# Codes of four later chunks from the normalised tokens in place, with twice scaled weights

## The chip, the cores and the metric

The kernel runs on one core of one Trainium2 chip. The metric is the device time of one execution in microseconds (us); lower is better. TensorE, VectorE, ScalarE, GpSimd and SyncE are called PE, DVE, ACT, POOL and SP in the profile. PEld is TensorE's weight loading, which runs beside its products.

## The reference, cut to what matters

The input is normalised, and then goes through an RWKV-6 attention layer and a mixture of experts; both results are added to the input. The part that the change touches is the start of the attention layer, the low-rank codes:

```
xn     = layernorm(x)                      # 4 x 1024 tokens, 256 channels
x_last = concatenate([zeros, xn[:, :-1]])  # the token before
b_a    = x_last - xn
xx     = xn + b_a * miu_x                  # mixed tokens
h      = tanh(xx @ A).reshape(5, B * T, 32)
```

`A` has 256 rows and 160 columns (five groups of 32). The reshape lays the products out so that token t's five codes come from different tokens. Everything behind `h` (five mixtures, decay, key, value, receptance, gate, the recurrence, the output and the experts) is left as it is.

## The kernel before, in words

The normalised tokens lie in SBUF with channels on the partitions, in two halves of 128 channels (`xnT`, a view of `xnf`), each sequence with a zero column ahead of it. The attention part goes through eight chunks of 128 tokens, each in two units of two sequences; a unit is written (u, c). Each engine has its own program, a list of steps written out by hand, and semaphores order the engines against each other. An engine takes its steps strictly in the written order. The first stretch, to about 130 us, interleaves the codes of all chunks with the units (0,0), (1,0) and (0,1) and with the routing of tokens to experts; behind it the loop `half` takes one unit and its share of the 39 expert tiles per turn.

The codes of chunk c go as follows.

- ACT, `scaled(c)` (L1355): two instructions, one for each half of the channels, write `xn * (1 - miu_x)` for 20 strips of 28 tokens (560 columns) into one of two buffers `xxb`. It waits for the products of the chunk before last (`s["hm"]`).
- DVE, `shifted(c)` (L845): two instructions add `x_last * miu_x` in place. That makes the mixed tokens of the chunk.
- ACT, `codes(c)` (L1383 and L1388): tanh into `codes_f`, then a rounded copy into `codes_hl`.
- DVE, `low_codes(c)` (L866): the remainder of the rounding. SP then writes the codes to memory, from where they are loaded for each unit.

The other steps that the prediction speaks of: on PE `mixed(u, c, n)` (L435) forms the five mixtures' factors from the codes, `decay_down` (L446), `decay_up` (L459), `key` (L466, `wk`), `value` (L482), `receptance` (L466, `wr`), `gate_down` (L498), `first_levels` (L515), `middle_levels` and `last_levels` (L525, L556), `key_back` (L570), `read_out` (L590, L594), `state` (L605), `table` (L406), `gated_back` (L630). On DVE `mixed` (L1024) and `added` (L1032) form the mixtures, `grow` (L1085 to L1087) and `levels` (L1054, L1063) belong to the recurrence, `places_of_tiles` (L964 to L978) and `at_rows` (L982) to the routing, `key` is L1040. On ACT `decay_down` is L1411, `decay` L1419 and `gate_down` L1442.

The order around the change, on PE: `first_levels(0,0)`, `mixed(1,0,1)`, `codes(3)`, `decay_down(1,0)`, `mixed(1,0,2)`, `decay_up(1,0)`, `middle_levels(0,0)`, `key(1,0)`, `codes(4)`, `mixed(1,0,3)`, `value(1,0)`, `last_levels(0,0)`, `mixed(1,0,4)`, `receptance(1,0)`, `codes(5)`, `gate_down(1,0)`, `mixed(0,1,0)`, `first_levels(1,0)`, `mixed(0,1,1)`, `key_back(0,0)`, `codes(6)`, `decay_down(0,1)`, `state(0,0)`, `mixed(0,1,2)`, `read_out(0,0)`, `codes(7)`, `decay_up(0,1)`, `table(0)`.

The waits of `codes(c)` on PE, and the view of the strips:

```
def tokens_of(c, cc, shift):
    at = PAD + cc * ROWS + BASE[c] + shift - 1
    return xnf[:, at:at + NB * (T + 1)].rearrange("p (s n) -> p s n", n=PITCH)[:, :, 0:SEG]
...
pe.wait_ge(s["xx"], c + 2)
...
    pe.wait_ge(s["h"], c if c > 5 else c - 1)
```

`SEG` is 28 and `PITCH` 205: a chunk's strips are 20 runs of 28 tokens, 205 apart. `wA` lies in `z`, `xxb` and the codes' buffers in the first part of `w1`, which holds the experts' first weights later. Their load (SP, L1889) waits until all codes are written out.

Of the kernel before, what the change touches and what calls it, by code (L numbers as in the profile page):

```python
# [11 lines left out]
ACT = mybir.ActivationFunctionType  # L12
AX = mybir.AxisListType

P = 128
NB, T, C = 4, 1024, 256
TOK = NB * T
CC = C // P
# [52 lines left out]

NSEG, PITCH, SEG = NB * NS, (NB * (T + 1)) // (NB * NS), 28
SHIFT = [4 + (P * c - 4) % NS for c in range(NCH)]
BASE = [(P * c + NS - f) // NS for c, f in enumerate(SHIFT)]
# [24 lines left out]
def program(nc, io):  # L101
    with ExitStack() as ctx:
        def sb(name, shape, dt=F32):
# [77 lines left out]

        s = {n: ctx.enter_context(nc.semaphore("s_" + n)) for n in (

            "cv cn c1 c2 w x0 x1 x2 x3 x4 x5 x6 x7 xk ck0 ck1 ck2 z_pool omx bn ag ve rs nm xna xnd xnp tr tc sc lg xx hm h hi lo "
            "four hg hf hc cx ls lgc lgt bst cst wvc ew1 ew2 "

            "step exp cnt slot att ohp inv back srow drow ex "
# [13 lines left out]
        def cvec(col, cc):  # L201
            return vec[:, col + cc:col + cc + 1]
# [30 lines left out]
        HAT = FAT + 2 * TC5  # L233
        codes_f = [w1[:, FAT + TC5 * k:FAT + TC5 * (k + 1)] for k in range(2)]
        codes_hl = [w1[:, HAT + 2 * NS * P * k:HAT + 2 * NS * P * (k + 1)].rearrange("p (x i n) -> p x i n", x=2, i=NS) for k in range(3)]
        lgs = w1s[:, 0, :, :].rearrange("p k n -> p (k n)")[:, 0:NT * E]
        wA = flat(z)[:, 0:CC * GR].rearrange("p (c n) -> p c n", c=CC)
        wA4 = D[:, :, :].rearrange("p u n -> p (u n)")[:, 0:CC * GR * 4].rearrange("p (a m) -> p a m", m=P)
# [22 lines left out]
# [4 lines that stand above are left out]
        def codes_in(c, cc):  # L265
            return xxb[c % 2][:, cc, :].rearrange("p (s n) -> p s n", n=SEG)

        def half_of(strips, u):
            return strips.rearrange("p (s b) n -> p s b n", b=NB)[:, :, UB * u:UB * (u + 1), :]
# [27 lines left out]
        def home(c):  # L297
            return YB if c in (0, 2, 4) else F2
# [36 lines left out]
        def tensor_program(pe):  # L335
# [41 lines left out]

            def codes(c):

                pe.wait_ge(s["xx"], c + 2)  # L380
                if c == 0:
                    pe.wait_ge(s["hf"], 2)
                elif c == 1:
                    pe.wait_ge(s["hf"], NS)
                else:
                    pe.wait_ge(s["h"], c if c > 5 else c - 1)
                for g in range(NS):
                    for cc in range(CC):
                        for t in range(NB):
                            i1 = pe.matmul(home(c)[LORA * t:LORA * (t + 1), g * GAP:g * GAP + GSEG], wA[:, cc, LORA * g:LORA * (g + 1)],  # L390
                                           xxb[c % 2][:, cc, t * GSEG:(t + 1) * GSEG], start=(cc == 0), stop=(cc == 1), tile_position=(0, LORA * t))
                i1.then_inc(s["hm"])

            def counts():
# [424 lines left out]
        def vector_program(dve):  # L819
# [21 lines left out]

            def shifted(c):
                for cc in range(CC):
                    dve.wait_ge(s["sc"], CC * (c + 1) + cc + 1)
                    i1 = dve.scalar_tensor_tensor(codes_in(c, cc), tokens_of(c, cc, 0), cvec(MX, cc), codes_in(c, cc), ALU.mult, ALU.add)  # L845
                i1.then_inc(s["xx"])

# [381 lines left out]
            tiles_of_experts()  # L1229
            mixed(1, 0, 0)  # L1230
            low_codes(2)
            shifted(3)
            grow(0, 0, 1)
            dve.wait_ge(s["z_pool"], 3)
            levels(0, 0, 0)
# [5 lines left out]
            mixed(1, 0, 2)  # L1241
            grow(0, 0, 4)
            low_codes(3)
            shifted(4)
            grow(0, 0, 8)
            added(1, 0, 2)
            levels(0, 0, 2, 3)
# [14 lines left out]
            slots()  # L1262
            low_codes(5)
            mixed(0, 1, 0)
            shifted(6)
            added(0, 1, 0)
            gate_terms(1, 0)
            mixed(0, 1, 1)
            places_of_tiles()
            low_codes(6)  # L1270
            shifted(7)
            added(0, 1, 1)
            mixed(0, 1, 2)
            at_rows(0)
# [59 lines left out]
        def scalar_program(act):  # L1334
# [7 lines left out]
            def columns(j):  # L1342
                act.wait_ge(s["tr"], j + 1)
                for cc in range(CC):
                    i1 = act.activation(xrow(j, 1)[:, cc, :], pair_of(j)[cc][:, :], ACT.Copy)
                i1.then_inc(s["tc"])
# [10 lines left out]
            def scaled_half(u):  # L1357
                act.wait_ge(s["tc"], NJ - 1 + u)
                act.wait_ge(s["xna"], NJ - 1)
                act.wait_ge(s["xnd"], NJ - 1)  # L1360
                act.wait_ge(s["xnp"], NJ - 1)
                for cc in range(CC):
                    act.activation(half_of(codes_in(0, cc), u), half_of(tokens_of(0, cc, 1), u), ACT.Copy, scale=omx[:, cc:cc + 1]).then_inc(s["sc"])

            def four_copies():
                act.wait_ge(s["c1"], 48)
# [39 lines left out]
            def decay_down(u, c):  # L1406
                q = seq(u, c)
                act.wait_ge(s["tA"], q + 1)
                if q:
                    act.wait_ge(s["tB"], q)  # L1410
                act.activation(tw[:, :], bank(u, c, "tw")[:, 0:P], ACT.Tanh).then_inc(s["tw"])  # L1411
# [203 lines left out]
            scaled(1)  # L1615
            act.wait_ge(s["w"], 208)
            decay_down(0, 0)
            decay(0, 0)
            exponentials()
            codes(1)  # L1620
# [3 lines left out]
            receptance(0, 0)  # L1624
            bonus(0, 0)
            codes(2)
            scaled(3)
            gate_down(0, 0)
            saved(0, 0, 2)
            saved(0, 0, 4)  # L1630
            codes(3)
            decay_down(1, 0)
            scaled(4)
            decay(1, 0)
            saved(0, 0, 16)
            saved(0, 0, 32)
# [5 lines left out]
            receptance(1, 0)  # L1642
            bonus(1, 0)
            codes(5)
            scaled(6)
            gate_down(1, 0)
            spread(0, 0)
            key_back(0, 0)
            codes(6)
            scaled(7)  # L1650
            decay_down(0, 1)
            squares(0, 0)
            codes(7)
# [308 lines left out]
```

## Time and profile before

| | us |
|---|---|
| median of 3 runs | 579.27 (577.48 to 579.47) |
| the profiled execution, its own time | 581.6 |
| its span in the profile | 580.3 |
| PE busy | 527.7 (91% of the span) |
| PEld busy | 469.8 (81%) |
| DVE busy | 449.1 (77%) |
| ACT busy | 338.5 (58%) |
| POOL busy | 195.1 (34%) |

The span runs from the first to the last instruction; the execution's own time is 1.3 us longer. Busy time is the union of an engine's instructions. In a row of the timeline, instructions that follow each other on one line are merged: the columns are start, duration, engine, line, operation, output and inputs, count, and in brackets the idle time ahead of them with what ended it. A merged row's end can reach past the next row's start, since instructions overlap in the pipeline. In a row of a window, the granted TensorE clock stands behind the engines' busy times: 1.00 is 2.4 GHz, 0.50 is 1.2 GHz.

### The profile page before, as it was taken

The numbers are of one execution on the slowest core, as the hardware profiler recorded it, in microseconds if no ns is written. First come the engines' busy times: TensorE is split into PE (matmuls) and PEld (weight loads), VectorE is DVE, ScalarE is ACT, GpSimd is POOL, SyncE is SP. The second block draws the span as 40 slices with busy tenths as digits, with TensorE's granted clock in tenths as the row PEclk, the third lists the DMA queues.
The fourth block names the chain that finished last, engine by engine and source line by source line (L and its number), as shares of the span: only waits on it lengthen the run. The fifth ranks groups of instructions, "written<-read, shape, count | busy, mean of one in ns | idle before, by whom it ended". The sixth has DMA issues, their size and how long they took to land. (4 is left out here: it accounts for less than half of the span.)

```text
span 580.3 us, 19573 instructions
## 1 busy us (share of the span) xinstructions
PE 527.7 (91%) x7662; PEld 469.8 (81%) x7662; DVE 449.1 (77%) x1116; ACT 338.5 (58%) x753; POOL 195.1 (34%) x156
## 2 busy tenths in 40 slices
PE   2879796987999999999999899999998999989984
PEld 2667586876898999998998799999997889878873
DVE  6879999977869596968697787869676868878552
ACT  4975564324575756566666557575746666565751
POOL 7901010130324334434243232524333523423332
PEclk9999899997999999999999999999999999999999
DMA  8989654579332434324233323242433433221323
GB/s 281 265 298 306 171 137 102 148 274 322 88 72 39 96 47 94 56 75 75 73 62 89 46 72 51 57 81 43 99 47 75 74 76 56 48 38 39 38 39 46
DMA packets 49805, 60.80 MB, mean 105 GB/s; under 512 B 5057, under 2 KB 44098, under 8 KB 49570
## 3 DMA queue, kind: packets, MB, share of 16 engines
q1 hardware_dynamic: 36898, 44.72, 27.0%
q0 software_dynamic: 11840, 14.42, 16.6%
q8 instruction: 62, 1.02, 0.8%
q10 hardware_dynamic: 976, 0.41, 0.3%
q14 instruction: 29, 0.24, 0.1%
HBM read 40.79 MB, written 23.07 MB: 110 GB/s over the span
## 5 line engine op out<-in xcount | busy, mean ns | idle before, releaser
L1742 POOL DMA_INDIRECT out<-rows,dst_row x39 | 63.9, 1637 | 214.3 <-DVE rows L1153 187.6
L661 PE MATMUL F<-xsT,w1s 128*128 128x128 f32 x624 | 76.8, 276 | 2.5 <-issue 1.4
L661 PEld LDWEIGHTS F<-xsT,w1s 128*128 128x128 f32 x624 | 74.7, 192 | 4.8 <-issue 1.8
L1024 DVE SCALAR_TENSOR_TENSOR mix<-G,vec,ba 128x256 f32<-128x256 f32 x160 | 69.6, 477 | 11.4 <-PE G L435 11.3
L669 PE MATMUL F<-w,hsT 128*128 x312 | 75.1, 383 | 0.5 <-ACT hsT L1542 0.3
L1542 ACT ACTIVATE hsT<-F,b1c 128x128 f32<-128x128 f32 x156 | 44.4, 369 | 35.3 <-PE F L661 31.4
L669 PEld LDWEIGHTS F<-w,hsT 128*128 128x128 f32 x312 | 57.2, 190 | 8.8 <-issue 0.9
L1063 DVE COPY_PREDICATED AP_<-msk,LL 128x256 f32<-128x256 uint32 x96 | 51.2, 534 | 16.3 <-issue 11.0
L1085 DVE TENSOR_TENSOR RK<-RK,D 128x256 f32<-128x256 f32 x112 | 47.4, 423 | 19.0 <-issue 10.7
L1032 DVE TENSOR_TENSOR mix<-mix,xnT 128x512 f32<-128x512 f32 x80 | 55.1, 688 | 1.5
L1728 POOL DMA_INDIRECT rows<-xn_d,src_row x39 | 40.8, 1046 | 33.5 <-PE F L650 16.6
L1153 DVE SCALAR_TENSOR_TENSOR rows<-F,of_row,b2t 128x256 f32<-128x256 f32 x39 | 18.6, 477 | 41.3 <-PE F L669 41.2
L1086 DVE TENSOR_TENSOR RK<-RK,D 128x256 f32<-128x256 f32 x112 | 46.9, 419 | 0.0
L1535 ACT ACTIVATE w1s<-w 128x1024 f32 x39 | 41.7, 1069 | 3.5 <-issue 3.5
L435 PE MATMUL G<-cd,bst 128*128 128x256 f32 x160 | 40.2, 338 | 1.9 <-ACT tg L1442 1.0
L1720 POOL TENSOR_TENSOR gn<-gn,small 128x8 f32<-128x8 f32 x16 | 28.3, 1771 | 39.0 <-DVE gn L1120 38.9
L1466 ACT ACTIVATE D<-RK 128x256 f32<-128x256 f32 x32 | 13.8, 430 | 41.7 <-DVE D L1087 41.6
L1716 POOL TENSOR_TENSOR ba<-xnT 128x512 f32<-128x512 f32 x16 | 18.4, 1152 | 55.7 <-DVE mix L1024 55.5
L1524 ACT ACTIVATE xsT<-F 128x256 f32<-128x256 f32 x39 | 14.9, 381 | 31.8 <-PE F L650 31.4
L466 PE MATMUL G<-mix,wk 128*128 128x256 f32 x128 | 31.4, 389 | 2.2 <-ACT D L1419 2.2
L482 PE MATMUL G<-wv,mix 128*128 128x256 f32 x128 | 30.6, 381 | 2.8 <-DVE RK L1040 2.8
L1748 POOL DMA_DIRECT2D out<-res x16 | 21.2, 1326 | 34.4 <-DMA out<-rows,dst_row 34.4
(181 smaller groups left out, 1216.0 us busy)
## 6 DMA issues: line engine op xcount, KB each, us to landing
cd<-cd_d SPq DMA_DIRECT2D x30, 320.0 KB, 5.2
w<-in_W SPq DMA_DIRECT2D x16, 512.0 KB, 8.9
cd_d<-w SPq DMA_DIRECT2D x32, 160.0 KB, 2.8
b2t<-in_b SPq DMA_DIRECT2D x39, 128.0 KB
w<-in_x SPq DMA_DIRECT2D x8, 512.0 KB, 9.5
xn_d<-w SPq DMA_DIRECT2D x8, 512.0 KB
out<-in_x SPq DMA_DIRECT2D x8, 512.0 KB, 5.8
out<-res POOLq DMA_DIRECT2D x16, 256.0 KB
```

The source lines that it names most:

```text
L435: i1 = pe.matmul(bk[:, cc * UN:(cc + 1) * UN], bst[:, n, cc * P:(cc + 1) * P], cd[:, u, n, :].bitcast(F32R), start=True, stop=True)
L661: i1 = pe.matmul(FB[:, k * P:(k + 1) * P], w1s[:, cc, k, :], xsT[:, cc, :], start=(cc == 0), stop=(cc == 1))
L669: i1 = pe.matmul(FB[:, 0:C], hsT[:, k, :], w2[:, bass.ds(number[f] * (HC * C) + k * C, C)], start=(k == 0), stop=(k == HC - 1))
L1024: i1 = dve.scalar_tensor_tensor(mixed_in(u, c, n, cc), bk[:, cc * UN:(cc + 1) * UN], cvec(LAM + CC * n, cc), ba[:, cc, :, :].rearrange("p ...
L1032: dve.tensor_tensor(buf, buf, xunit(u, c, 1), ALU.add).then_inc(s["x"])
L1063: dve.copy_predicated(to, m, now.rearrange("p g (n t) -> p g n t", t=B)).then_inc(s["a"])
L1085: dve.tensor_tensor(r2, r2, bcast(tt[:, :, 0], B), ALU.mult)
L1086: dve.tensor_tensor(k2, k2, bcast(tt[:, :, 1], B), ALU.mult)
L1535: act.activation(w1s[:, :, :, :].rearrange("p c k n -> p (c k n)"), w1[:, bass.ds(n * (CC * HID), CC * HID)], ACT.Copy).then_inc(s["fw"])
L1542: i1 = act.activation(hsT[:, k, :], FB[:, k * P:(k + 1) * P], ACT.Relu, bias=b1c[:, bass.ds(number[f] * HC + k, 1)])
L1728: pool.indirect_dma_start(xs[:, f % 2, :], None, xn_d, bass.IndirectOffsetOnAxis(src_row[:, f:f + 1], 0)).then_inc(s[f"xs{f % 2}"], 16)
L1742: pool.indirect_dma_start(io["out"], bass.IndirectOffsetOnAxis(dst_row[:, f:f + 1], 0), ys[:, f % 2, :], None, compute_op=ALU.add).then_in ...
```

## The change

For the chunks 3, 4, 6 and 7 (`DIRECT`) no mixed tokens are formed. The sum `xn * (1 - miu_x) + x_last * miu_x` is not taken before the product but in it: `wA` is kept in two more versions, `wAs`, one scaled by `miu_x` and one by `1 - miu_x`, and PE multiplies the first with the strips one token back and the second with the strips themselves, both read from the normalised tokens in place. An accumulation group has four products where it had two, so such a chunk has 80 matmuls (160 records) where it had 40 (80). The chunks 1, 2 and 5 (`STRIPS`) and chunk 0 stay as they are. `scaled` and `shifted` of the four chunks are gone from ACT and DVE; `weights_of_strips` is new on ACT, with four instructions between `decay_down(0, 0)` and `decay(0, 0)`. No DMA, no step of POOL and no step of SP changes.

```
+DIRECT = (3, 4, 6, 7)
+STRIPS = [c for c in range(1, NCH) if c not in DIRECT]
...
+        SAT = HAT + 3 * 2 * NS * P
+        wAs = w1[:, SAT:SAT + 2 * CC * GR].rearrange("p (x c n) -> p x c n", x=2, c=CC)
...
-                pe.wait_ge(s["xx"], c + 2)
+                if c in DIRECT:
+                    pe.wait_ge(s["ws"], 2 * CC)
+                else:
+                    pe.wait_ge(s["xx"], 3 + STRIPS.index(c) if c else 2)
...
-                for g in range(NS):
-                    for cc in range(CC):
-                        for t in range(NB):
-                            i1 = pe.matmul(home(c)[LORA * t:LORA * (t + 1), g * GAP:g * GAP + GSEG], wA[:, cc, LORA * g:LORA * (g + 1)],
-                                           xxb[c % 2][:, cc, t * GSEG:(t + 1) * GSEG], start=(cc == 0), stop=(cc == 1), tile_position=(0, LORA * t))
+                def columns(w, of, n):
+                    for g in range(NS):
+                        for m in range(n):
+                            for t in range(NB):
+                                i1 = pe.matmul(home(c)[LORA * t:LORA * (t + 1), g * GAP:g * GAP + GSEG], w(m)[:, LORA * g:LORA * (g + 1)],
+                                               of(m, t), start=(m == 0), stop=(m == n - 1), tile_position=(0, LORA * t))
+                    return i1
+
+                if c in DIRECT:
+                    i1 = columns(lambda m: wAs[:, m // CC, m % CC, :], lambda m, t: tokens_of(c, m % CC, m // CC)[:, NS * t:NS * (t + 1), :], 2 * CC)
+                else:
+                    i1 = columns(lambda m: wA[:, m, :], lambda m, t: xxb[c % 2][:, m, t * GSEG:(t + 1) * GSEG], CC)
                 i1.then_inc(s["hm"])
...
-                    dve.wait_ge(s["sc"], CC * (c + 1) + cc + 1)
+                    dve.wait_ge(s["sc"], CC * (2 + STRIPS.index(c)) + cc + 1)
...
             low_codes(2)
-            shifted(3)
             grow(0, 0, 1)
...
             low_codes(3)
-            shifted(4)
             grow(0, 0, 8)
...
             mixed(0, 1, 0)
-            shifted(6)
             added(0, 1, 0)
...
             low_codes(6)
-            shifted(7)
             added(0, 1, 1)
...
+            def weights_of_strips():
+
+                for cc in range(CC):
+                    act.activation(wAs[:, 0, cc, :], wA[:, cc, :], ACT.Copy, scale=cvec(MX, cc)).then_inc(s["ws"])
+                    act.activation(wAs[:, 1, cc, :], wA[:, cc, :], ACT.Copy, scale=omx[:, cc:cc + 1]).then_inc(s["ws"])
...
             decay_down(0, 0)
+            weights_of_strips()
             decay(0, 0)
...
             codes(2)
-            scaled(3)
             gate_down(0, 0)
...
             decay_down(1, 0)
-            scaled(4)
             decay(1, 0)
...
             codes(5)
-            scaled(6)
             gate_down(1, 0)
...
             codes(6)
-            scaled(7)
             decay_down(0, 1)
```

How the change stands on the engines, at two places. On PE, from `mixed(1,0,1)` to the start of `decay_down(1,0)`, with the products of chunk 3 between; before:

```order
L435 MATMUL G<-cd,bst 128x256 [waits s_tg]
L435 MATMUL G<-cd,bst 128x256
L390 MATMUL F<-w,z 32x140 [waits s_h,s_xx]
L390 MATMUL F<-w,z 32x140 x39
L446 MATMUL G<-mix,tdA 64x128 [waits s_m,s_x]
```

and with the change:

```order
L449 MATMUL G<-cd,bst 128x256 [waits s_tg]
L449 MATMUL G<-cd,bst 128x256
L398 MATMUL F<-xnT,w 32x140 [waits s_h,s_ws]
L398 MATMUL F<-xnT,w 32x140 x79
L460 MATMUL G<-mix,tdA 64x128 [waits s_m,s_x]
```

The step stands where it stood, has twice as many matmuls, reads `xnT` with the weights in `w`, and waits no longer for DVE (`s_xx`) but for the scaled weights (`s_ws`). The other three chunks read alike.

On DVE, around `places_of_tiles` and the strips of chunk 7 (L845 here), before:

```order
L974 TENSOR_TENSOR w<-rows,placef 128x32x39 [waits s_tr,s_xk,s_slot]
L976 TENSOR_TENSOR w<-w,prob 128x32x39 [waits s_att]
L978 TENSOR_TENSOR w<-w,rows 128x32x39 [waits s_att]
L866 TENSOR_TENSOR w<-w 128x640 [waits s_ck0,s_hi]
L845 SCALAR_TENSOR_TENSOR w<-xnT,vec,w 128x560 [waits s_sc] x2
L1032 TENSOR_TENSOR mix<-mix,xnT 128x512 [waits s_m]
```

and with the change (lines are 14 further down):

```order
L988 TENSOR_TENSOR w<-rows,placef 128x32x39 [waits s_tr,s_xk,s_slot]
L990 TENSOR_TENSOR w<-w,prob 128x32x39 [waits s_att]
L992 TENSOR_TENSOR w<-w,rows 128x32x39 [waits s_att]
L880 TENSOR_TENSOR w<-w 128x640 [waits s_ck0,s_hi]
L1046 TENSOR_TENSOR mix<-mix,xnT 128x512 [waits s_m]
```

Only the two instructions on the strips are gone; what stood behind them follows directly. All steps that stay keep their order on every engine.

## Rows read from the trace of the kernel before

**Rows 1.** The page's part 1: busy time of each engine over the whole span.

```profile
PE 527.7 (91%) x7662; PEld 469.8 (81%) x7662; DVE 449.1 (77%) x1116; ACT 338.5 (58%) x753; POOL 195.1 (34%) x156
```

**Rows 2.** Windows: stretch, its length, busy PE, PEld, DVE, ACT, POOL, granted clock, DMA.

```profile
60.27:103.41 43.14, 35.08 (x758) 29.83 (x762) 41.42 (x83) 21.89 (x41) 1.55 (x1) 0.92 0.50 133
69.00:73.00 4.00, 4.00 (x96) 3.62 (x90) 3.47 (x8) 1.21 (x4) 0.00 (x0) 0.57 0.61 132
104.90:126.60 21.70, 20.17 (x238) 18.24 (x238) 21.07 (x50) 6.85 (x17) 3.25 (x3) 1.00 0.82 256
133.00:134.00 1.00, 1.00 (x14) 1.00 (x16) 1.00 (x4) 0.47 (x1) 0.00 (x0) 0.50 1.04 367
220.00:280.00 60.00, 60.00 (x859) 54.62 (x859) 46.49 (x115) 38.16 (x89) 22.15 (x17) 1.00 0.36 71
```

**Rows 3.** Timeline of PE around the products of the chunks 3, 4, 6 and 7.

```profile
60.27 0.50 PE L435 MATMUL G<-cd,bst 128*128 128x256 f32 x2 [0.48 <-ACT tg L1442]
61.64 2.59 PE L390 MATMUL F<-w,z 128*32 128x140 f32 x80 [0.86 <-DVE w L845]
65.53 0.66 PE L446 MATMUL G<-mix,tdA 128*64 128x128 f32 x8 [1.30 <-DVE mix L1032]
67.92 0.67 PE L459 MATMUL G<-tw,tdB 64*64 64x128 f32 x16 [1.10 <-DVE mix L1024]
...
73.75 2.47 PE L390 MATMUL YB<-w,z 128*32 128x140 f32 x76
...
76.27 0.51 PE L435 MATMUL G<-cd,bst 128*128 128x256 f32 x2
...
90.35 2.59 PE L390 MATMUL F<-w,z 128*32 128x140 f32 x80 [1.23 <-DVE w L845]
92.87 0.66 PE L446 MATMUL G<-mix,tdA 128*64 128x128 f32 x8
...
95.97 0.40 PE L594 MATMUL YB<-V,AT 128*64 128x64 f32 x8
99.18 4.23 PE L390 MATMUL F<-w,z 128*32 128x140 f32 x80 [2.80 <-DVE w L845]
```

**Rows 4.** Timeline of DVE: strips of chunk 3, and the waits behind it.

```profile
60.07 1.51 DVE L845 SCALAR_TENSOR_TENSOR w<-xnT,vec,w 128x560 f32<-128x560 f32 x2
61.50 0.42 DVE L1085 TENSOR_TENSOR RK<-RK,D 128x256 f32<-128x256 f32 x1
...
76.82 0.88 DVE L1024 SCALAR_TENSOR_TENSOR mix<-G,vec,ba 128x256 f32<-128x256 f32 x2 [0.48 <-PE G L435]
...
103.36 0.42 DVE L1087 TENSOR_TENSOR D<-D 128x256 f32<-128x256 f32 x1
105.00 0.83 DVE L866 TENSOR_TENSOR w<-w 128x640 fp32r<-128x640 f32 x1 [1.22 <-ACT w L1388]
...
129.81 0.43 DVE L1085 TENSOR_TENSOR RK<-RK,D 128x256 f32<-128x256 f32 x1 [3.24 <-PE LL L525]
```

**Rows 5.** Timeline of ACT: the place of the new instructions, and steps near the change.

```profile
40.75 0.28 ACT L1411 ACTIVATE tw<-G 128x128 f32<-128x128 f32 x1 [0.24 <-PE G L446]
43.06 0.84 ACT L1419 ACTIVATE D<-G,vec 128x256 f32<-128x256 f32 x2 [2.04 <-PE G L459]
...
58.31 1.43 ACT L1355 ACTIVATE w<-xnT,small 128x560 f32<-128x560 f32 x2
59.64 0.58 ACT L1442 ACTIVATE tg<-G 128x512 f32<-128x512 f32 x1
...
103.45 0.75 ACT L1383 ACTIVATE w<-F 128x700 f32<-128x700 f32 x1 [6.43 <-PE F L390]
104.23 0.74 ACT L1388 ACTIVATE w<-w 128x640 fp32r<-128x640 f32 x1
```

**Rows 6.** Timeline of PE: products whose moving operand is in one run, and in pieces of 8.

```profile
149.81 0.65 PE L525 MATMUL LL<-Ru,AT 64*64 64x32 f32 x32
150.28 0.65 PE L525 MATMUL LL<-RK 64*64 64x32 f32 x32
```

More of the change, by code:

```diff
@@ L182, in program @@
         s = {n: ctx.enter_context(nc.semaphore("s_" + n)) for n in (
-            "cv cn c1 c2 w x0 x1 x2 x3 x4 x5 x6 x7 xk ck0 ck1 ck2 z_pool omx bn ag ve rs nm xna xnd xnp tr tc sc lg xx hm h hi lo "
+            "cv cn c1 c2 w x0 x1 x2 x3 x4 x5 x6 x7 xk ck0 ck1 ck2 z_pool omx bn ag ve rs nm xna xnd xnp tr tc sc ws lg xx hm h hi lo "
             "four hg hf hc cx ls lgc lgt bst cst wvc ew1 ew2 "
```

## The prediction

> **What bounds the kernel now.** The page's part 1 comes first: over the whole span PE is busy for 91% [rows 1]. Then the windows, since that share is an average [rows 2]. From 220 to 280 us PE is busy for all of 60.00 us while DVE has 46.49: the loop behind the change is bound by PE, so whatever moves the loop's start moves the end by as much. The stretch with the four products, from 60.27 to 103.41 us, is another matter: PE is busy for 35.08 of 43.14 us, DVE for 41.42. Part of PE's work there also runs slowly: from 69 to 73 us the granted clock is 0.57 on average. Behind it, from 104.90 to 126.60, DVE is busy for 21.07 of 21.70 us and sets the pace.
>
> The timeline of PE shows what the 8.06 us of idle PE were waiting for [rows 3]. The products of chunk 3 waited 0.86 us for the strips from DVE, those of chunk 6 1.23, those of chunk 7 2.80. Those of chunk 4 did not wait. Between them PE waited for DVE's mixtures (1.30 and 1.10 us) and twice about half a microsecond for ACT's gate tanh (0.48 in the row, once more ahead of chunk 6). So this stretch is a loop of dependencies between PE and DVE in which both are nearly full, and the change moves work from the fuller of the two to the other.
>
> **What it adds.** A chunk's 80 records take 2.59 us at full clock [rows 3], 32.4 ns each, and the next step starts as they end (76.27, 92.87). So a direct chunk takes 160 records, 5.18 us, and four of them add 4 x 2.59 = 10.4 us to PE. No row shows this product with its moving operand read in runs of 28. I price it at 32.4 ns. The other end is 52.9 ns, from the 4.23 us of chunk 7 at reduced clock.
>
> **What it takes away.** On DVE a pair of strip instructions keeps the engine for 61.50 - 60.07 = 1.43 us [rows 4]; four pairs are 5.7 us. On ACT a pair is 1.43 busy, with the gate tanh starting 1.33 us behind its start [rows 5]; four pairs are 5.3 us. ACT is not full, so only the two places count where the tanh stood behind a pair, chunks 3 and 6.
>
> **The scaled weights.** Four ACT instructions of 128x160. The nearest rows are 0.28 us for 128x128 and 0.42 each for the pair of 128x256, so 1.1 to 1.7 us, and they go into the 2.04 us in which ACT waits for PE between L1411 and L1419 [rows 5]. Cost zero; without this cover `decay(0,0)`, and PE's `key(0,0)` behind it, would come up to 1.7 us later. The wait on `ws` is over some 15 us before chunk 3.
>
> **The stretch, step by step** (before, then after, in us).
>
> - Chunk 3. Without `scaled(3)`, ACT's tanh is no longer late, PE's `mixed(1,0,1)` starts at 59.8 instead of 60.27 and the products at 60.3 instead of 61.64. They end at 65.5 instead of 64.2. DVE, 1.4 us earlier, has the mixture for `decay_down(1,0)` ready at 64.1, so this starts at 65.5, as before (65.53). `decay_up(1,0)` waits for `mixed(1,0,2)` on both engines and comes at 67.5 instead of 67.92. The doubled products have filled PE's waits.
> - The clock. From 69 to 73 us the mean grant was 0.57 [rows 2], so 0.43 x 4.00 = 1.7 us of full-speed work were lost. PE had been idle for 3.3 us of the 8 before (the three waits above). With the direct products those 8 us have some 1.5 idle, and I take it that the clock stays up. From `decay_up(1,0)` to the products of chunk 4 it was 73.75 - 67.92 = 5.8 us; less 1.7 that is 4.1, from 67.5 to 71.6.
> - Chunk 4 had no wait to fill [rows 3]: 71.6 to 76.8, where it ended at 76.3. So `mixed(1,0,3)` comes 0.5 us late. DVE waited for it even before (0.48 at 76.82 [rows 4]); now it waits over 2 us, which is where the time won from chunks 3 and 4 on DVE is lost again. From there to the strips of chunk 6 both engines run 0.5 us late.
> - Chunk 6. DVE drops a pair and is 0.9 us ahead. On PE, `mixed(0,1,1)` no longer waits for the tanh, so the lag of 0.5 is gone and `key_back` ends at 89.1. The products start at 89.1 instead of 90.35 and end at 94.3 instead of 92.9. PE is 1.4 us late: the step behind `read_out` can start at 97.5 instead of 96.15 (95.97 plus the 0.2 us after which a row's last products let the next step begin, as the rows around them show).
> - Chunk 7 starts there, at 97.5 instead of 99.18. Before, it fell to half clock right behind the 2.80 us of waiting, and took 4.23 us. With no wait ahead of it I take full clock: 5.18 us, ending at 102.7 instead of 103.41.
> - Next in line are ACT's two steps (L1383, L1388; rows 5) and DVE's `low_codes(7)`, which waited 1.22 us for them at 105.00 [rows 4]. They come 0.7 us earlier. DVE, which gets there at 101.4 rather than 103.8 (+0.5 of lag, -2.9 for the pairs of chunks 6 and 7), spends the rest waiting. From here DVE sets the pace to 126.6, the writing of chunk 7's codes and the loading of the experts' weights behind it follow, and the whole shifts by -0.7.
>
> As a sum over PE: 10.4 added; 4.9 of waits for strips, 1.0 of waits for the tanh and 1.9 of other waits filled; 1.7 and 1.6 of clock given back (4.23 - 2.59). That leaves -0.7. The span becomes 580.3 - 0.7 = 579.6, with the 1.3 us around it 580.9, against 581.6 of the profiled execution. That execution was 2.3 us over the median of 579.27; against the median the forecast is **578.6**. A measurement of this kernel tells about 0.5% (2.9 us) from no change.
>
> **A rule weighed.** In 60.27 to 103.41 PEld is busy for 29.83 us (69%), PE for 35.08, DVE for 41.42 (96%) [rows 2]. The Trainium skill, Perfetto Trace Analysis, Identifying the Most-Contended Engine, says that matmul busy time does not tell how near TensorE is to its limit, that weight loading's busy share should be read for it, and that the engine with the highest occupancy is to be relieved first. By that TensorE has room, the change relieves the right engine and the sum would be near -5.7 instead of -0.7. The trace speaks against the room: the products of a chunk and the step behind them stand end to end [rows 3].
>
> **The rivals.**
>
> - **The clock stays low.** The half-speed stretches have another cause than PE's waits, and come back at the same length: 1.7 and about 1.6 us lost again. Then chunk 4 ends at 78.5 and the end is at -0.7 + 3.3 = +2.6, which is 581.9. For it: the first fall came behind waits of 1.30 us at most, the second behind 2.80. Against: from 220 to 280 us, with PE full, the grant is 1.00 throughout.
> - **The direct products cost more per record (slower).** The place is the 640 direct records. Each ns on top of 32.4 adds 0.64 us to PE, since nothing is left to fill; from 33.5 ns on the change loses, from 38 ns by over 0.5% (3.6 us / 640). At the bound of 52.9 ns it is 13.1 us, so 578.6 + 13.1 = 591.7. For it: the moving operand comes in runs of 28 from four places at once. Against: the recurrence's products with a moving operand in pieces of 8 take the 0.65 us of those in one run [rows 6].
> - **DVE is the bound** and PE takes the added records between others: -5.7, 573.6. It needs room on PE that the end-to-end steps don't show.
> - **A later stretch goes another way.** At 133 us the clock is at half again, and DVE waits 3.24 us for PE at 129.81 [rows 2, 4]. If the shift spares that, some 2 to 3 us go with it: about 576. Equally it could lengthen.
> - That the change doesn't do what it says: the order shows the eight DVE instructions gone and 80 matmuls in four places, so no chance is kept for it.
>
> **How the numbers follow.** Forecast 0.58. The clock stays low 0.15, of which 0.03 end above +0.5% (where it comes back longer). Direct records dearer 0.15, slower. DVE the bound 0.06, faster. A later stretch 0.06, faster. So faster 0.12, same 0.58 + 0.12 = 0.70, slower 0.18. The range reaches down to the forecast less the spread of the runs and part of the last rival, 575.8, and up past the low clock, 582.8. Outside are the bound by DVE and most of the dearer records.
>
> **What would show it.** Right: 160 records in 5.2 us for each of the four chunks, no waits for DVE ahead of them, a granted clock of 1.00 from 60 to 103 us, chunk 4's products ending about 0.5 us later and chunk 7's about 0.7 earlier than before, a new DVE wait of over 2 us for PE near 75 and one near 102. Wrong: a direct chunk above 6 us at full clock, grants near 0.5 inside 60 to 103, or a loop that starts more than 3 us from where it did.

## The result and the profile after

The changed kernel takes 584.17 us (median of 4 runs, 583.56 to 586.42) against 578.77 of the kernel before beside it (4 runs, 577.48 to 579.47). The ratio is 1.0089, with a 95% interval from 1.0052 to 1.0127: **slower by 0.9%**, 5.4 us, where 578.6 had been forecast. In a second comparison (e5, below) it was 1.0073 (1.0042 to 1.0105). The profiled execution took 584.46 us for a span of 583.2. Medians in us are over all executions; a ratio leaves out those over 1.5% above the fastest of the same kernel (two of six in e1, one of six in e2).

Part 1 of the page after, beside [rows 1]: PE has 320 records more and 7.5 us more of busy time, DVE 5.3 us less, ACT 3.6 less.

```profile
PE 535.2 (92%) x7982; PEld 476.5 (82%) x7982; DVE 443.8 (76%) x1108; ACT 334.9 (57%) x749; POOL 195.7 (34%) x156
```

ACT's timeline shows the four scaled weights (L1378, L1379) in the wait that had been named for them [rows 5]. Of the wait 0.77 us are left, so they cost nothing.

```profile
41.34 0.28 ACT L1427 ACTIVATE tw<-G 128x128 f32<-128x128 f32 x1 [0.24 <-PE G L460]
41.51 0.42 ACT L1378 ACTIVATE w<-z,vec 128x160 f32<-128x160 f32 x1
...
42.47 0.41 ACT L1379 ACTIVATE w<-z,small 128x160 f32<-128x160 f32 x1
43.66 0.84 ACT L1435 ACTIVATE D<-G,vec 128x256 f32<-128x256 f32 x2 [0.77 <-PE G L473]
```

PE's timeline after, beside [rows 3]. The direct products are the rows of L398 with x160.

```profile
44.64 3.55 PE L480 MATMUL G<-mix,wk 128*128 128x256 f32 x8 [1.04 <-ACT D L1435]
...
61.18 0.89 PE L529 MATMUL LL<-Ru,RK 64*64 64x96 f32 x32
...
62.43 5.37 PE L398 MATMUL F<-xnT,w 128*32 128x140 f32 x160
67.73 0.66 PE L460 MATMUL G<-mix,tdA 128*64 128x128 f32 x8
...
71.61 0.67 PE L539 MATMUL LL<-RK 64*64 64x32 f32 x30
74.25 0.24 PE L539 MATMUL LL<-RK 64*64 64x32 f32 x2 [1.97 <-issue]
74.42 2.70 PE L480 MATMUL G<-mix,wk 128*128 128x256 f32 x8
77.05 6.03 PE L398 MATMUL YB<-xnT,w 128*32 128x140 f32 x160
83.01 0.50 PE L449 MATMUL G<-cd,bst 128*128 128x256 f32 x2
...
95.22 5.13 PE L398 MATMUL F<-xnT,w 128*32 128x140 f32 x160
100.28 0.66 PE L460 MATMUL G<-mix,tdA 128*64 128x128 f32 x8
...
103.72 5.11 PE L398 MATMUL F<-xnT,w 128*32 128x140 f32 x160
108.77 0.67 PE L473 MATMUL G<-tw,tdB 64*64 64x128 f32 x16
```

Two things are to be seen. No direct product waits for anything, and at full clock 160 records take 5.11 to 5.37 us. And in the middle levels (L539) PE stands for 1.97 us between the 30th and the 31st of 32 records, with nothing named that it waited for. The windows after give the clock: half at 45 to 48 us and again from 75.5 to 79, right behind that standstill, in which no engine did anything (73 to 74).

```profile
45.00:48.00 3.00, 3.00 (x9) 2.34 (x8) 1.72 (x4) 0.42 (x1) 0.00 (x0) 0.50 1.32 343
60.27:69.00 8.73, 8.55 (x209) 7.12 (x207) 7.41 (x18) 4.06 (x9) 0.00 (x0) 1.00 0.75 217
73.00:74.00 1.00, 0.00 (x0) 0.00 (x0) 0.00 (x0) 0.00 (x0) 0.00 (x0) 1.00 0.21 51
75.50:79.00 3.50, 3.50 (x41) 2.42 (x43) 3.40 (x9) 1.44 (x4) 0.00 (x0) 0.51 0.61 176
```

DVE's timeline, beside [rows 4], has the two new waits that were forecast, at 83.55 and 110.48, and ahead of them a third of 3.33 us, for the products at which PE stood.

```profile
74.60 0.42 DVE L1099 TENSOR_TENSOR RK<-RK,D 128x256 f32<-128x256 f32 x1 [3.33 <-PE LL L539]
...
83.55 0.88 DVE L1038 SCALAR_TENSOR_TENSOR mix<-G,vec,ba 128x256 f32<-128x256 f32 x2 [3.87 <-PE G L449]
...
110.48 0.82 DVE L880 TENSOR_TENSOR w<-w 128x640 fp32r<-128x640 f32 x1 [2.68 <-ACT w L1404]
```

This last instruction stood at 105.00 before: 5.5 us late. They add up as follows. `first_levels` started at 61.18 instead of 58.90: +2.3. Of that 0.6 stood already at 41 us (ACT's tanh at 41.34 instead of 40.75 [rows 5]), and 1.7 are the half clock behind it, in `key(0, 0)` at 44.64 above all (3.55 us for its 8 records). From there to `decay_up(0, 1)` it was 44.4 us before (58.90 to 103.33), 43.7 by the forecast (58.9 to 102.6), and 47.6 after: 3.9 more than forecast. The standstill is 1.97 of that, the half clock from 75.6 to 79.0 another 1.7.

That these 5.5 us are as large as the difference of the medians is chance. The two profiled executions differ by 2.9 us at their end (spans of 583.2 and 580.3), since the kernel before lost more behind it: from 126 to 142 us its granted clock was 0.79 on average, and 0.89 after, which is 3.4 against 1.8 us of full-speed work. The rows are the kernel before and the changed one.

```profile
126.00:142.00 16.00, 12.00 (x215) 10.50 (x215) 8.82 (x26) 5.87 (x12) 3.60 (x3) 0.79 0.90 276
126.00:142.00 16.00, 12.59 (x188) 10.96 (x187) 11.47 (x33) 6.93 (x15) 3.60 (x3) 0.89 0.79 229
```

### The profile page after: what moved, and what is told of

Same layout as the page of the kernel before. It is cut to its first block and busy times, and to the rows that moved or that the text cites. A ratio compares the mean times of both kernels' runs of the same rounds, so it can differ in the third digit from the quotient of the medians.

```text
span 583.2 us, 20201 instructions
## 1 busy us (share of the span) xinstructions
PE 535.2 (92%) x7982; PEld 476.5 (82%) x7982; DVE 443.8 (76%) x1108; ACT 334.9 (57%) x749; POOL 195.7 (34%) x156
## 3 DMA queue, kind: packets, MB, share of 16 engines
q8 instruction: 64, 1.05, 0.8%
## 5 line engine op out<-in xcount | busy, mean ns | idle before, releaser
L675 PE MATMUL F<-xsT,w1s 128*128 128x128 f32 x624 | 76.9, 276 | 2.1 <-ACT xsT L1540 1.4
L675 PEld LDWEIGHTS F<-xsT,w1s 128*128 128x128 f32 x624 | 74.7, 192 | 4.7 <-ACT xsT L1540 1.6
L683 PE MATMUL F<-w,hsT 128*128 x312 | 75.2, 383 | 0.6 <-ACT hsT L1558 0.3
L683 PEld LDWEIGHTS F<-w,hsT 128*128 128x128 f32 x312 | 57.1, 190 | 9.1 <-issue 1.2
L1558 ACT ACTIVATE hsT<-F,b1c 128x128 f32<-128x128 f32 x156 | 44.4, 368 | 34.8 <-PE F L675 34.7
L1167 DVE SCALAR_TENSOR_TENSOR rows<-F,of_row,b2t 128x256 f32<-128x256 f32 x39 | 18.6, 477 | 43.5 <-PE F L683 43.5
L480 PE MATMUL G<-mix,wk 128*128 128x256 f32 x128 | 33.0, 404 | 2.2 <-ACT D L1435 2.2
L651 PE MATMUL YB<-wo,sq 128*128 128x256 f32 x128 | 30.7, 381 | 2.2 <-issue 1.5
```

The costliest lines, as they stand in the source:

```text
L675: i1 = pe.matmul(FB[:, k * P:(k + 1) * P], w1s[:, cc, k, :], xsT[:, cc, :], start=(cc == 0), stop=(cc == 1))
L683: i1 = pe.matmul(FB[:, 0:C], hsT[:, k, :], w2[:, bass.ds(number[f] * (HC * C) + k * C, C)], start=(k == 0), stop=(k == HC - 1))
L1558: i1 = act.activation(hsT[:, k, :], FB[:, k * P:(k + 1) * P], ACT.Relu, bias=b1c[:, bass.ds(number[f] * HC + k, 1)])
```

## The experiments

In all of them the edit is against the changed kernel, whose diff stands above.

### The two halves of the change, each alone (e1, e2)

**e1** lets each accumulation group of a direct chunk stop after two of its four products, so the codes of the chunks 3, 4, 6 and 7 lack the part of the tokens themselves: DVE and ACT are relieved, and PE keeps its 80 records per chunk.

```
-                    i1 = columns(lambda m: wAs[:, m // CC, m % CC, :], lambda m, t: tokens_of(c, m % CC, m // CC)[:, NS * t:NS * (t + 1), :], 2 * CC)
+                    i1 = columns(lambda m: wAs[:, m // CC, m % CC, :], lambda m, t: tokens_of(c, m % CC, m // CC)[:, NS * t:NS * (t + 1), :], CC)
```

> The changed kernel with the products of chunks 3, 4, 6 and 7 cut to half (80 records a chunk, those with the token before alone; the half with the token itself is left out). ACT and DVE are relieved as in the change, PE has no added records. Working theory (VectorE's 5.7 us come back where it sets the pace, and PE's added 10.4 us are what eats them): 3 to 6 us faster than the kernel before, no wait of these products for DVE, no idle of PE marked issue around 72 us. Rival (the stretch is bound by PE and by fixed points such as the routing, so relief alone brings nothing): within 1 us of the kernel before.

Measured: 575.93 us against 580.33 (ratio 0.9893, 0.9843 to 0.9942). The stretch from `first_levels` to `decay_up(0, 1)` takes 37.3 us. The direct form with one run of 80 records takes 2.67 us, as the products of strips do, and PE waits for DVE again behind it:

```profile
61.73 2.67 PE L398 MATMUL F<-xnT,w 128*32 128x140 f32 x80
65.67 0.66 PE L460 MATMUL G<-mix,tdA 128*64 128x128 f32 x8 [1.26 <-DVE mix L1046]
```

**e2** forms and awaits the strips of all chunks as before, and multiplies the four chunks directly all the same.

```
-DIRECT = (3, 4, 6, 7)
+DIRECT = ()
...
-                if c in DIRECT:
+                if c in (3, 4, 6, 7):
...
+            shifted(3)
...
+            scaled(3)
...
```

`shifted` and `scaled` of the chunks 4, 6 and 7 come back in the same way, and so do the waits of `codes` on `xx`.

> The kernel before with only PE's side of the change: direct products with 160 records for chunks 3, 4, 6 and 7, but the strips are still formed and still waited for, and the scaled weights are made. Working theory: the added records have no wait left to fill, so 8 to 11 us slower than before, less what DVE works on meanwhile; at the least 5. Rival (PE has room for the records between others, as the low share of weight loading would have it): within 2 us of before.

Measured: 588.32 us, 1.0118 (1.0079 to 1.0156), and 52.6 us for the stretch. The waits for strips stay and the long products come on top. PE's rows for the chunks 3 and 6:

```profile
62.77 5.46 PE L398 MATMUL F<-xnT,w 128*32 128x140 f32 x160 [0.81 <-DVE w L859]
...
98.60 5.13 PE L398 MATMUL F<-xnT,w 128*32 128x140 f32 x160 [1.22 <-DVE w L859]
```

So the change is a trade of two effects of several microseconds each: -4.4 us for the relief and +8.0 for the records by the medians, -6.2 and +6.8 by the ratios. PE did not take the added work for free. The rule of the Trainium skill (Perfetto Trace Analysis, Identifying the Most-Contended Engine), by which PEld's 69% left room on TensorE, would have given -5.7. e2 speaks against that room: with the waits for strips kept, the added records cost 6.8 to 8.0 us.

### Which chunks lose (e3, e11, e4, e7)

`DIRECT` says which chunks are direct; `scaled` and `shifted` of the others stand where they stood before. **e3**, and again **e11**: the chunks 6 and 7. **e4**: chunk 4. **e7**: chunk 3.

```
-DIRECT = (3, 4, 6, 7)
+DIRECT = (6, 7)
```

> Direct products for the chunks 6 and 7 alone; 3 and 4 as before. Both had waits for strips (1.23 and 2.80 us) and chunk 7 ran at half clock behind its wait (1.6 us lost), so by the step-by-step working 5.2 us are added and 5.6 + 0.5 taken away: 0 to 2 us faster than before. Theory that the loss sits in chunks 3 and 4 (a record more without a wait to fill, the idle issue of 2 us and the slow clock behind it): this kernel is at least 4 us faster than the changed one. Rival (the direct products cost their full time wherever they are): 2.5 us slower than before.

> The kernel with direct products for chunks 6 and 7 alone once more, on another visit, to see whether it beats the kernel before: it gave 0.996 (0.993 to 0.999). Theory 'waits filled': the two chunks filled 4.0 us of PE's waits of 5.2 added, and freed DVE and ACT, so 0.993 to 0.999 again. Rival 'the visit': the clock's falls and the stalls in PE's stream come where they come, and the ratio lies on both sides of 1.

> Direct products for chunk 4 alone. Its products did not wait for the strips before, so 2.6 us are added on PE and DVE's 1.43 us come back only where DVE is waited for next: 1 to 3 us slower than before. Rival (DVE is the bound behind it, so its relief counts in full): 1 us faster.

> Direct products for chunk 3 alone. By the step-by-step working they fill the waits of 0.86, 1.30 and 1.10 us and cost nothing, DVE is 1.4 us earlier: 0 to 2 us faster than before. Theory of the instruction stream: 160 records more ahead of the middle levels put an idle of 1.7 to 2 us at the same place as in the changed kernel (record 1693), so 0 to 2 us slower than before.

| direct chunks | us (runs) | before | ratio (95%) |
|---|---|---|---|
| 6, 7 (e3) | 578.83 (12) | 580.33 | 0.9958 (0.9927 to 0.9990) |
| 6, 7 (e11) | 578.70 (12) | 579.49 | 0.9992 (0.9969 to 1.0016) |
| 4 (e4) | 582.27 (12) | 580.33 | 1.0039 (1.0008 to 1.0070) |
| 3 (e7) | 581.82 (9) | 578.30 | 1.0057 (1.0027 to 1.0087) |

Chunks 6 and 7 pay for themselves: in e3 their products stand without a wait at full clock (`decay_up(0, 1)` follows at 104.86), where before 1.23 and 2.80 us of waiting stood ahead. Whether they gain more than that stays open, since the second comparison has 1 in its interval.

```profile
91.32 5.13 PE L398 MATMUL F<-xnT,w 128*32 128x140 f32 x160
...
99.82 5.11 PE L398 MATMUL F<-xnT,w 128*32 128x140 f32 x160
```

Chunk 3 was a surprise, since it has waits to fill. Both expectations missed it: 3.3 us slower by the ratio, where 0 to 2 had been the most, though the second named the standstill. Its profile shows the waits filled, and the same standstill as after, at the same two records of L539:

```profile
62.62 5.13 PE L398 MATMUL F<-xnT,w 128*32 128x140 f32 x160
...
73.92 0.32 PE L539 MATMUL LL<-RK 64*64 64x32 f32 x2 [1.70 <-issue]
```

The kernels with chunk 4 or chunk 3 alone share another one. It lies in the first pass of the loop, within `mixed` and far from anything edited; here in e4, at 151.70 in e7, and 2.27 us in both:

```profile
150.79 0.38 PE L449 MATMUL G<-cd,bst 128*128 128x256 f32 x1
153.44 0.38 PE L449 MATMUL G<-cd,bst 128*128 128x256 f32 x1 [2.27 <-issue]
```

### What the standstills follow (e5, e8, e6)

The records of PE and PEld ahead of each standstill were counted. In the four profiled executions in which chunk 3 is direct with 160 records and nothing is put ahead of it (after, e2, e5, e7), PE stands after record 1693, for 1.97, 1.70, 1.21 and 1.70 us. In the two kernels with one direct chunk it stands after record 3954. In the kernels with strips for chunk 3 (before, e3, e4) record 1693 is another place of the program, and in the middle levels ahead of chunk 4 PE runs through. That speaks for a place in PE's instruction stream as the cause of the standstill: the change adds 640 records of PE and PEld to it, and all that comes later is moved along it.

**e5** is the changed kernel once more, unedited; **e8** the kernel before, for one profile.

> The changed kernel once more, for a second profile and more times beside the runs of this call. Theory of the instruction stream (TensorE's idle marked issue sits at fixed positions of its own instruction stream, not at a time): the idle of about 2 us comes again after record 1693 of products and weight loads together, in the products L539 of the middle levels, as it did in the kernel with PE's side alone, which has the same stream; the time is 3 to 6 us over the kernel before. Rival (it was an accident of one execution): no idle marked issue over 0.5 us between 60 and 110 us, and a time within 2 us of the kernel before.

> The kernel before once more (the same instructions), for a second profile. Theory of the instruction stream: idle marked issue after the records 11665 and 12502, as in the first profile and in the kernel with relief alone. Theory on the clock (where it falls varies from one execution to the next): a fall between 44 and 49 us, which the first profile of before did not have and all others had, or another place than 69 to 73 us. Rival: the clock falls at the same places as in the first profile.

e5: 582.06 us (9 runs) against 578.30, 1.0073 (1.0042 to 1.0105). Its PE rows have the standstill but no half clock behind it:

```profile
71.50 0.67 PE L539 MATMUL LL<-RK 64*64 64x32 f32 x30
73.38 0.24 PE L539 MATMUL LL<-RK 64*64 64x32 f32 x2 [1.21 <-issue]
73.55 1.99 PE L480 MATMUL G<-mix,wk 128*128 128x256 f32 x8
75.48 5.13 PE L398 MATMUL YB<-xnT,w 128*32 128x140 f32 x160
```

Its stretch is 45.0 us: the 43.7 of the forecast and the 1.21. Behind the longer standstills the clock did fall: at 75.6 us in the first profile, at 74.0 in e2 and at 73.6 in e7, each time to half for at least 3.4 us.

In e8 (581.95 us) the windows show the kernel before with the half clock at 45 to 48 us, and the full one at 69 to 73, where the profile that the prediction was read from had it the other way round [rows 2].:

```profile
45.00:48.00 3.00, 3.00 (x9) 2.38 (x8) 1.62 (x5) 0.42 (x1) 0.00 (x0) 0.50 1.29 334
69.00:73.00 4.00, 3.09 (x116) 2.79 (x117) 4.00 (x10) 2.23 (x5) 0.00 (x0) 1.00 0.24 52
```

Its stretch is 42.8 us, 1.6 shorter than in that profile. Of the two standstills expected in it the one after record 11664 came (1.37 us), the one after 12502 did not.

**e6** puts 128 records of PE and PEld (32 products that nobody reads) at the head of PE's stream, so that everything else lies 128 records further on.

```
+            pe.wait_ge(s["cn"], 16)
+            for _ in range(32):
+                pe.matmul(LL[:, 0:32], ident, con[:, IDN:IDN + 32], start=True, stop=True)
             for j in range(NJ):
                 ln_transpose(j)
```

> The changed kernel with 32 small products (64 records, 64 weight loads) at the head of TensorE's stream, where it waits 10 us for the tokens anyway; their result is written over. Theory of the instruction stream: the idle of 2 us in L539 at record 1693 goes away or moves to another place by 128 records, and if the new place is harmless the kernel is 1.5 to 3.5 us faster than the changed one. Rival (the idle comes from the density of the products before it, 160 direct ones and 96 of the levels): it stays in L539, and the time stays.

The standstill was gone and the stretch took 43.5 us, but the 64 PE records ran for 13.86 us at about 217 ns each and delayed the start by some 7 us. So the time, 588.10 us, tells nothing of the standstill's worth:

```profile
4.93 13.86 PE L738 MATMUL LL<-con 128*128 128x32 f32 x64 [4.93 <-DMA con<-in_con]
...
79.04 0.68 PE L539 MATMUL LL<-RK 64*64 64x32 f32 x32
```

### The same shift without its price (e9, e10, e12)

The pad is 32 products with 32 columns of weights, on zeros that are in place at 1.5 us. **e9** has it in the changed kernel, **e10** in the kernel before, **e12** in the kernel with the chunks 6 and 7 direct.

```
+            pe.wait_ge(s["z_pool"], 2)
+            for _ in range(32):
+                pe.matmul(LL[0:32, 0:32], hsT[:, 0, 0:32], hsT[:, 0, 0:32], start=True, stop=True)
             for j in range(NJ):
                 ln_transpose(j)
```

> The changed kernel with 32 small products of zeros (32 columns of weights, 32 moving columns, 64 PE records with 64 weight loads) at the head of PE's stream, where PE waits until 9.97 us anyway; nothing of the computation changes. It repeats the padded kernel without the late start: the pad may run from 1.5 us and should be over by 8 or 9 us, so first_levels should stay near 61.2 us. Theory 'the place in PE's stream': the 1.2 to 2.0 us in which PE stood in the middle levels at the same record of the stream (in all executions of the changed kernel) are gone, or under 0.6 us, because other records now lie at that place; decay_up(0,1) then starts within 45.5 us of first_levels (43.5 in the padded kernel, 47.6 and 45.0 in the two of the changed one), and the time is 1 to 2.5 us below the changed kernel: 1.002 to 1.006 of before. Rival 'the wait belongs to the middle levels themselves (a transfer or an engine that the trace does not name)': PE stands there as long as before, and the time is that of the changed kernel, 1.007 to 1.009. A miss is possible where another place of the stream moves into a full stretch.

> Control: the kernel before with the same 32 small products of zeros at the head of PE's stream. If the pad is free, the span is that of before within 1 us, apart from the stalls: the kernel before has none over 0.3 us ahead of 127 us and 1.15 us at 127.8 to 129.3. Theory 'the place in PE's stream': the stalls of before come at other instructions, each 128 records earlier in the program, and the time moves by less than 0.4% either way. Rival 'the pad itself costs or wins (clock at the start, a later start)': first_levels starts more than 1 us away from 58.9 to 61.0 us, or the time moves by over 0.5%.

> Direct products for chunks 6 and 7 alone with the 32 small products of zeros at the head of PE's stream. The unpadded one showed PE standing 1.38 us near record 5028 and 2.63 us near record 15228 with no releaser. Theory 'the place in PE's stream': both standings leave the instructions at which they were and come elsewhere or not at all, and the time moves by up to 2 us either way against the unpadded one of this job. Rival 'they belong to the instructions': PE stands at the same instructions (the same line, tile and chunk) for as long.

| kernel, 12 runs each | us | ratio to before (95%) |
|---|---|---|
| changed, padded (e9) | 580.33 | 0.9998 (0.9970 to 1.0026) |
| before, padded (e10) | 580.09 | 1.0013 (0.9986 to 1.0040) |
| chunks 6 and 7, padded (e12) | 580.00 | 1.0017 (0.9991 to 1.0044) |

With the pad the changed kernel is no slower than the one before, with or without the pad, and its interval doesn't meet that of e5. That is more than the 1.002 to 1.006 expected. Of the 13 executions of the changed kernel above none took under 580.8 us; of the 12 padded ones four took 575.0 to 576.6. On the time of the kernel before the pad shows no effect. It isn't without one in the profiles, though: e10 and e12 have the half clock from about 8 to 18 us, which no other profile has. PE's timeline of e9: the pad is over at 5.1 us, where PE would have waited until 9.97, and the 32 records of L539 run through.

```profile
1.49 3.62 PE L738 MATMUL LL<-hsT 128*32 128x32 f32 x64 [1.49 <-POOL hsT L1791]
...
70.46 0.68 PE L539 MATMUL LL<-RK 64*64 64x32 f32 x32
71.07 1.99 PE L480 MATMUL G<-mix,wk 128*128 128x256 f32 x8
73.00 5.13 PE L398 MATMUL YB<-xnT,w 128*32 128x140 f32 x160
```

The window of e9 from `first_levels` to `decay_up(0, 1)` is 43.54 us at a granted clock of 1.00:

```profile
60.29:103.83 43.54, 42.35 (x1107) 37.97 (x1107) 37.67 (x78) 18.78 (x36) 1.55 (x1) 1.00 0.50 129
```

The profiles of e5 and e9 don't show where the time was won. e9 has no standstill and no half clock in the stretch, and at `decay_up(1, 1)` it is 4.1 us ahead of e5 (135.81 against 139.90) and 6.5 ahead of the first profile of the changed kernel. But then PE waits for the last transfer of the experts' second weights (landed at 149.25 us), and the clock falls to half behind it (0.91 on average from 142 to 160 us). The kernel before does the same in e8, where it is as early (135.79; landed at 149.91). The rows are e9 and e8; in before, after, e5 and e10, which come there 3.6 to 6.5 us later, L683 waits for nothing and takes 1.89 us.

```profile
149.50 3.63 PE L683 MATMUL F<-w,hsT 128*128 x8 [1.80 <-DMA w<-in_W]
150.16 3.31 PE L683 MATMUL F<-w,hsT 128*128 x8 [2.48 <-DMA w<-in_W]
```

At the end the profiled execution of e9 (581.46 us) is 0.4 us longer than that of e5 (581.06). It is also the longest of e9's twelve, and e5's is one of the shortest of its nine. What the shorter executions do differently no profile shows.

e12 is a caution. The 1.38 and 2.63 us that e3 and e11 both show after the records 5028 and 15228 are gone from their places there, as expected, but 1.38 us turned up after record 12112 and 0.83 after 7142, and the time did not fall. e10 likewise shows 1.51 us near record 12020, at `output` (L651), which the kernel before had not. The pad moved such places; it didn't remove them.

### What PE waited for

The profile has a DMA queue named "instruction", which brings 64 packets to the changed kernel, 1.05 MB in all: 16 KB each, one for each 250 or so of the 15964 records of PE and PEld. The DMA view of the changed kernel from 71.5 to 71.7 us (first the window in 40 slices, then the queue: packets, MB, share of 16 engines) catches the start of one:

```profile
DMA  0000000000000000000000000009000000000000
...
q8 instruction: 1, 0.02, 40.6%
```

It starts in slice 28, at 71.63 us. 40.6% of 16 engines for 0.2 us are 1.30 us, so it ends at 72.93, and PE goes on at 74.25, **1.32 us later**. The same sum gives 1.38 us in e5, 1.37 in e2 and 1.42 in e7 for this place, 1.59 and 1.50 for the one after record 3954, and 1.27 to 1.38 for the one at L651 (after, e2, e10). So PE stood until 2.4 to 2.8 us behind the start of the packet, for what the records it still had did not cover: 57 at 71.63 us here, 2 in e4, and 167 in e5, which has the shortest of the standstills. Why these packets came too late isn't shown. They started 302 to 372 records after the ones before, where about 250 are the mean, but in the changed kernel others started 375, 449 and 451 records after (at 153.94, 259.21 and 383.10 us) and PE ran through. The standstills ahead of `hidden` (L675, 1.38 and 2.63 us) don't fit: there PE resumes 2.7 to 4.8 us behind the last packet.

The Trainium skill (Runtime: NRT & Kernel Launch, Instruction fetch mechanics) says that the instructions come in blocks of 16 KiB by a DMA queue of the sequencer and that the cost is mostly hidden. The size agrees with the 16 KB here. Mostly hidden agrees too (2 of 64 packets in the changed kernel cost more than 1 us), but those two cost more than the edit's forecast effect.

## Why the prediction was wrong

- **The scaled weights, the added records:** right. Nothing on ACT's path, 5.11 to 5.37 us for a direct chunk at full clock against 5.18, with a median record of 284 ns where a strip's has 283. The rival of dearer records has fallen, and DVE as the bound as well (two waits for PE of over 2 us, as forecast: 2.23 and 2.65 in e9).
- **Chunks 3, 4, 6 and 7, step by step:** right, where PE's stream runs through. Forecast were 43.7 us from `first_levels` to `decay_up(0, 1)`; e9 and e6 have 43.5, e5 45.0 with its 1.21 of standstill. As a gain it holds only against an execution whose clock falls at 69 us (44.4 in the profile read and in e10). Against e8, which has 42.8, the change loses 0.7 us in this stretch.
- **The clock:** right as a mechanism, within this stretch. Of seven profiles with strips for chunk 3 six show a fall at 69 to 71 us, and e8 none. Of the four with the whole change (after, e5, e6, e9) none shows one there, and e9 holds 1.00 for the 43.54 us. What was wrong was to take the entry from one execution: 13 of the 14 profiles, of either kind, fall to half clock between 42 and 50 us (e6, delayed, at 50 to 57), and the one the prediction was read from doesn't. That is 1.7 us of the 5.5 in the comparison of the two traces, and e8 shows it without the change. The 1.7 us "given back" at 69 us are likewise no term of every execution, as e8 shows. The rival "the clock stays low" put its 1.7 us down to another cause than was seen: the fall at 75.6 in the after trace came behind the standstill, not behind PE's waits for DVE.
- **The sum, and the step that failed:** "That leaves -0.7" counted PE's new records by their duration alone. It had no term for the instruction stream that they lengthen by 640 records of PE and PEld. With them PE stood 1.2 to 2.0 us in the middle levels, at a place where an instruction packet came late, and in three of the four profiles that show it a fall of the clock followed, which cost at least another 1.7. Moving the stream by 128 records brings 1.0073 to 0.9998. That is 4.3 us by the ratios and 2.9 by the medians over the kernel before (3.8 and 0.8), from two comparisons made apart. By -0.7 us the forecast ratio was 0.9988, inside e9's interval.
- **The way to the end:** "the whole shifts by -0.7" and "whatever moves the loop's start moves the end by as much" don't hold between 127 and 160 us. Up to 142 us the clock fell for 6.8 us in before, for 3.4 in after and e5, and not at all in e8 and e9, which at 147.7 us waited 2.48 and 1.80 us for the experts' weights. The rival "a later stretch goes another way" named this place and gave it a chance on the faster side alone. In the pair of the first profiles it took 2.6 us off the loss.
- **What stays open.** That a shift of the stream takes the loss away is measured; that it does so by this one standstill is not. The pad moves every later packet too, and it has PE work at the start, where it would have waited. Only one length of it was tried on the changed kernel without a late start, so these can't be told apart. The standstill is 1.2 to 2.0 us and the clock fall behind it 1.7 where there is one, but in the profile of e9 the wait for weights takes what is won. Why a packet comes late wasn't found either.

## What to carry to other kernels

When an edit changes how many instructions an engine issues, and the expected gain is a few microseconds, look at the DMA queue of instructions and at idle time without a releaser before you believe either sign: shift the engine's stream with cheap instructions in a wait, in both kernels, and compare again. And take what the clock does from several executions: a fall that one profile shows in one place may stand 25 us earlier in the next. A gain ahead of a loop can also end in a wait that was covered before, here for the experts' weights, so read how far it gets. And longer products in place of a formed operand were level or a little better here only in chunks 6 and 7, where they filled the waits that this operand had made; chunk 3 alone cost 3.5 us and chunk 4 alone 1.9.

## What was not expected of the hardware

- PE stood idle with no releaser at the same record of its stream in several executions (1.21 to 1.97 us after record 1693 in four, 1.38 and 2.63 us after 5028 and 15228 in both of e3 and e11), and at record 1693 went on 1.32 to 1.42 us behind the end of a 16 KB packet on the instruction queue. The one after record 12532 was there in after and e2 and missing in e5.
- The first products of a program were slow, at a granted clock of 1.00: 64 records with 128 columns of weights took 13.86 us (217 ns each, e6), 64 with 32 columns 3.62 us (57 ns each, e9).
- A matmul whose moving operand comes in runs of 28 from four places costs what one from a single strip costs: 284 against 283 ns at the median, 32 ns from one to the next on average.
